# One wait a batch of eight in TensorE's adjacency loop, and one-hot slots of 392 columns in place of 391

## The reference, cut to what matters

```python
edge_index = jnp.stack([src, dst])            # 50000 edges, sorted by dst; 3125 nodes, 128 features
# first network: five gated steps
def step(h, _):
    messages = h[col] @ W_msg.T + b_msg
    agg = jax.ops.segment_sum(messages, row, num_segments=num_nodes)
    ...                                       # gates r, z, n of agg and h
x = _layernorm(x + gated_steps(x))
x = _layernorm(x + edge_network(x, edge_weight))   # three edge layers
```

## Time and profile before

| | us |
|---|---|
| median of 3 runs | 2377.35 (2377.28 to 2377.51) |
| the profiled execution, its own time | 2376.61 |
| the profiled execution, span of its instructions | 2374.4 |
| PE busy in the span | 2020.9 |
| DVE busy | 1455.5 |
| POOL busy | 1063.3 |
| ACT busy | 662.9 |
| adjacency stage: first to last matmul start | 74.1 to 375.7 |
| last staged copy of the stage, opening of the next stage | 379.87, 386.15 |

### The profile page before, as it was taken

One profiled execution on the slowest core, in us unless ns is written; L12 is line 12 of the kernel. 1 busy time (PEld: TensorE's weight loads), 2 busy tenths in 40 slices (PEclk: granted clock), 3 DMA queues, 4 the chain that ended last, 5 costly groups with the idle time before them and its releaser, 6 DMA issues. The chain is left out here.

```text
span 2374.4 us, 50364 instructions
## 1 busy us (share of the span) xinstructions
PE 2020.9 (85%) x14516; PEld 1445.6 (61%) x14516; DVE 1455.5 (61%) x4548; ACT 662.9 (28%) x1344; POOL 1063.3 (45%) x1086
## 2 busy tenths in 40 slices
PE   7687776999999997398888866999999769999983
PEld 4221113454544543287777755999999659888881
DVE  6888873132322323687878846767777467777774
ACT  0145663121211211332333324323233231111111
POOL 0444430000000000377777736777777267777770
PEclk7767767999999998699999978999999889999996
DMA  3022445000000001544444425777777345555541
GB/s 91 14 49 67 87 83 47 0 0 0 0 0 0 0 0 44 209 132 142 143 145 142 144 77 136 210 209 207 209 205 210 93 127 146 146 140 144 142 121 30
DMA packets 188937, 242.83 MB, mean 102 GB/s; under 512 B 53217, under 2 KB 115068, under 8 KB 188076
## 3 DMA queue, kind: packets, MB, share of 16 engines
q1 hardware_dynamic: 155420, 173.31, 25.4%
q0 software_dynamic: 32864, 60.32, 11.1%
q10 hardware_dynamic: 432, 6.29, 0.6%
HBM read 150.92 MB, written 69.26 MB: 93 GB/s over the span
## 5 line engine op out<-in xcount | busy, mean ns | idle before, releaser
L1504 POOL DMA_INDIRECT rows<-p_dram,src_i x912 | 893.0, 979 | 305.1 <-issue 257.4
L1737 DVE TENSOR_TENSOR agg_t<-psum,agg_t 128x128 f32 x1368 | 390.2, 285 | 153.2 <-PE psum L1621 122.9
L1603 PE MATMUL psum<-w_c,before 128*128 128x128 f32 x1824 | 403.6, 303 | 0.0
L1672 ACT ACTIVATE rows<-rows 128x512 f32<-128x512 f32 x228 | 143.7, 630 | 754.6 <-DVE rows L1730 750.5
L884 PE MATMUL psum<-adj,parts 128*128 (+2 forms) x1750 | 339.7, 351 | 5.6 <-ACT agg L963 4.4
L1721 DVE TENSOR_SCALAR hot_w<-col_f,dst_loc,weight 128x128 f32<-128x128 f32 x912 | 319.1, 354 | 0.3
L664 PE MATMUL psum<-src_hot,dst_hot 128*128 128x391 f16 x586 | 228.0, 432 | 81.3 <-ACT psum L686 27.5
L1603 PEld LDWEIGHTS psum<-w_c,before 128*128 128x128 f32 x1824 | 279.7, 194 | 0.0
L1264 POOL MEMSET agg_t<- 128x3200 f32 x1 | 2.8, 2766 | 606.5 <-POOLq L1020 606.5
L1621 PE MATMUL psum<-hot_w,rows 128*128 128x128 f32 x1824 | 247.3, 279 | 29.8 <-ACT rows L1672 25.8
L884 PEld LDWEIGHTS psum<-adj,parts 128*128 128x128 f16 x1750 | 153.0, 98 | 191.1 <-issue 23.4
(11 more groups left out here) (249 smaller groups left out, 2504.3 us busy)
## 6 DMA issues: line engine op xcount, KB each, us to landing
e_dram<-after SPq DMA_DIRECT2D x228, 256.0 KB
before<-e_dram SPq DMA_DIRECT2D x228, 256.0 KB
adj<-stage SPq DMA_DIRECT2D x196, 97.8 KB, 3.5
pair_rows<-sorted_rows SPq DMA_DIRECT2D x114, 128.0 KB, 4.3
rows<-p_dram,src_i POOLq DMA_INDIRECT x912
hot_all<-dst_rows SPq DMA_DIRECT2D x1, 3584.0 KB, 12.5
hot_all<-dst_rows ACTq DMA_DIRECT2D x1, 3072.0 KB, 17.3
hot_all<-dst_rows ACTq DMA_DIRECT2D x1, 2048.0 KB, 10.5
```

Of the source, the lines that this page charges most:

```text
L1504: nc.gpsimd.indirect_dma_start(out=rows[:, b % ROWS, m * D:(m + 1) * D], out_offset=None, in_=p_dram, in_offset=bass.IndirectOffsetOnAxis( ...
L1603: mm = nc.tensor.matmul(o, before[:, q % BEFORE, m * P:(m + 1) * P], w_c[:], start=False, stop=True)
L1672: nc.scalar.activation(e_of(q), source, ACT.Relu).then_inc(e_on, 1)
L1737: nc.vector.tensor_tensor(a, psum[:, A_BANKS[q % len(A_BANKS)], m * P:(m + 1) * P], a, ALU.add).then_inc(agg_on, 1)
```

## The change

The wait for the target batch is made only at the first step of a batch (74 of the 586). The source slots, and the ramp that they are compared with, get 392 columns; the matmul still reads 391 of them.

```diff
+SPAN_COLS = -(-SPAN // 4) * 4
...
-            keep["span_h"] = room[:, 2 * BAND_ROOM:3 * CHUNK].bitcast(F16)[:, 0:SPAN]
+            keep["span_h"] = room[:, 2 * BAND_ROOM:3 * CHUNK].bitcast(F16)[:, 0:SPAN_COLS]
...
-            nc.gpsimd.iota(keep["span_h"], [[1, SPAN]], 0, 0,
+            nc.gpsimd.iota(keep["span_h"], [[1, SPAN_COLS]], 0, 0,
...
-        src_hot = sb("src_hot", [P, MOVES, SPAN], F16)
+        src_hot = sb("src_hot", [P, MOVES, SPAN_COLS], F16)
...
-                pe.wait_ge(dst_on, s // HOT_BATCH + 1)
+                if s % HOT_BATCH == 0:
+                    pe.wait_ge(dst_on, s // HOT_BATCH + 1)
                 pe.wait_ge(src_on, s + 1)
                 pe.wait_ge(free, nth & 255)
                 nc.tensor.matmul(psum[:, bass.ds(bank, 1), 0:SPAN],
                                  dst_hot[:, s // HOT_BATCH % BATCHES, s % HOT_BATCH, :],
-                                 src_hot[:, s % MOVES, :], start=False, stop=False,
+                                 src_hot[:, s % MOVES, 0:SPAN], start=False, stop=False,
                                  skip_group_check=True).then_inc(counted, 1)
```

## The result

| | before, us | after, us |
|---|---|---|
| median | 2377.43 (4 runs) | 2347.06 (2346.03 to 2347.33, 4 runs) |
| profiled execution, its own time | 2376.61 | 2346.03 |
| its span | 2374.4 | 2343.8 |
| first matmul of the stage | 74.1 | 73.9 |
| last staged copy | 379.87 | 347.50 |

The ratio is 0.9869, with a 95% interval of 0.9857 to 0.988: 30.4 us saved, where 29.0 were forecast. Lines behind the change count two higher in the new kernel (L664 is L666, L677 is L679).

A forecast was written before the change was run, and what follows sets the result against it. TensorE's instruction issue bounds the stage's first half, ScalarE very nearly the second. Gain 30.9 - 0.5 - 1.4 = 29.0 us, so 2377.35 - 29.0 = 2348.4 us; range from 2 us below 2344.4 up to 2361.

The forecast's parts named there:

- TensorE is bound by issuing: Weight loads of L664: one every 0.41 to 0.42 us whatever the clock, set by sequencer instructions between loads.
- The price of the wait, 0.105 us at clock 1.0 and 0.089 at 0.5: TensorE's L662 wait: removing it saves this per step, 2.36 us per 28 steps, which fall from 14.22 to 11.86.
- the array's floor: TensorE's load-and-matmul of 391 columns at clock 0.5: no step shorter than 0.326 us.
- A lone wait needs no instruction: Ahead of L663: in 7 of 8 steps the L662 instruction goes, the remaining wait riding on L663's operation.
- ScalarE is next, from the block at 186 us on: Second half of the stage: ScalarE's 14-band blocks can't be shorter than 15.6 or 16.9 us.
- The deductions, 0.5 and 1.4 us: Taken off 30.9 us: VectorE holding TensorE in the first 28 steps, and TensorE and ScalarE delaying each other when level.
- seven blocks: ScalarE's 14-band blocks, 246.7 to 362.8 before: to take ScalarE's own 113.1 us instead of 116.1.
- its own range: Spread of the main forecast's total time: 2344.4 to 2352.8 us.
- level running: TensorE and ScalarE equally fast from about 186 us: each at times loses to the other, 1.4 us taken off.
- The 392 columns at zero: VectorE's source one-hots, L646: widening from 391 columns changes nothing; bounds 0.35 us lost or 0.5 us gained.
- Landings: Rival: staged bands' transfers take over at 0.90 us a band against 0.80, 13 us given back, 2361; chance 0.08.

The follow-up runs named there:

- the run where VectorE never paused: Changed kernel with ScalarE's band ends and TensorE's banks written in as constants, slots of 392 columns: 2844.21 us, ratio 1.0145 to the kernel before.
- the waits of VectorE: Added to the kernel with both engines' constants and 392 columns: VectorE waits each batch, from the third, for GpSimd's scatters; 2322.19 us, ratio 0.9766.

## Why the prediction was right, point by point

- **TensorE is bound by issuing.** Right. Of the three readings in it (the pace ignores the clock, the idle is "issue", the instructions between two loads add up) the two runs with added waits are the test: a second wait instruction moved the pace from 0.415 to 0.52. One figure was weaker than it was read: most of the idle in the 3.24 of 6.00 us is the gap of one register load, 2.56 us from the weight load at 127.80 to the next, and not idle between steps.
- **The price of the wait, 0.105 us at clock 1.0 and 0.089 at 0.5.** The first is right: 0.31 us within a batch, 74 wait instructions. Twenty-eight steps took (199.2 - 84.0) / 10 = 11.5 us between the loads of L655, where the forecast had 11.86 and, with 0.105 throughout, 11.65:

```profile
L655 PEldq TENSOR_LOAD <-band_i x11: 1874/2006/2518, 84.0 to 199.2; - x11
```

  The second was too low. In the stretch of the last row here, at a granted clock of 0.5, the loads still came 0.31 us apart, below the 0.326 that the prediction had as the array's floor:

```profile
88.48 0.10 PEld L666 LDWEIGHTS psum<-src_hot,dst_hot 128*128 128x128 f16 x1 [0.21 <-issue]
88.79 0.10 PEld L666 LDWEIGHTS psum<-src_hot,dst_hot 128*128 128x128 f16 x1 [0.20 <-issue]
89.10 0.10 PEld L666 LDWEIGHTS psum<-src_hot,dst_hot 128*128 128x128 f16 x1 [0.21 <-issue]
...
88.16:89.80 1.64, 1.64 (x6) 0.57 (x6) 0.50 0.25 61
```

  The floor seems to hold over a batch and not for each step: the eight loads from 88.16 on, with the slower first step of a batch among them, took 2.62 us (mean clock 0.55), and 8 x 0.326 is 2.61. By that estimate a batch at 0.5 saves 8 x 0.415 - 2.61 = 0.71 us, where the prediction had 7 x 0.089 = 0.62, and 28 steps save about 2.5 us and not 2.36. The other 0.2 us are not pinned down. The gap at a register load, from the last weight load before it to the first behind it, fell from a mean of 2.59 us (8 gaps before) to 2.46 (10 gaps after), less than single gaps differ by.

- **A lone wait needs no instruction.** Right, but the step's wording (one wait on the operation, "the other became" the instruction) hid a rule that the runs brought out: the wait instruction takes two. So taking one wait out of four ahead of an operation saves an instruction, out of three it saves none, and out of two, as in this kernel, it saves one.
- **ScalarE is next, from the block at 186 us on.** Right. The last load was forecast at 331.9 before deductions, and came at 330.3:

| ScalarE's load, before | forecast | after |
|---|---|---|
| 188.0 | 169.1 | 167.2 |
| 208.6 | 186.3 | 184.8 |
| 226.7 | 201.9 | 200.6 |
| 246.7 | 218.8 | 217.6 |
| 362.8 | 331.9 | 330.3 |

  The run without ScalarE's loads gave 31 us more, so the cap is shown and not only argued.
- **The deductions, 0.5 and 1.4 us.** Both were mis-sized. The 0.5 was too small: in the first 28 steps the loads that open the second, third and fourth batch came 0.85, 0.77 and 0.78 us after the one in front (76.17 to 77.02, 79.24 to 80.01, 82.21 to 82.99) in place of 0.41, so VectorE held TensorE for 1.2 us. The cheaper steps behind them more than made up for it. The 1.4 was a wrong reading: in the block from 296.1 to 314.4 ScalarE waited 0.99 us for a staged band to land, and that is most of the 1.4:

```profile
314.37 0.48 ACT L683 CAST stage<-psum 128x391 f16<-128x391 f32 x1 [0.99 <-DMA adj<-stage]
```

  Where no copy waited so, seven blocks took 112.7 us against my 113.1, in the changed kernel and in the run with the wait alone; with two such waits, in the changed kernel run again, they took 114.8. Two engines running level cost nothing that can be seen; a late landing does, in some executions. Without the deductions the forecast would have been 30.9 us, and the medians of the three pairs gave 30.4, 31.2 (the wait alone) and 31.5 (the changed kernel again). The total came out near for the right reason, ScalarE's own 113.1 us: what was wrong in TensorE's price moved only the point at which ScalarE takes over, by 1.5 us (184.8 against 186.3). The upper end of its own range was also added up wrongly: 29.0 less 3.0 for the seven blocks and less 2.8 for level running at three times its cost is 23.2, which gives 2354.2 and not 2352.8.
- **The 392 columns at zero.** Right, in a run of their own and where VectorE sets the pace. The Trainium skill's rule on 4-byte alignment (VectorE: DVE Perf Modes, section "Mode 2×_1P — pack two bf16 into one 32-bit read") would, as the prediction read it, have made every second slot of 391 slow; 2.98 and 2.99 us for a batch leave no room for that, so here the measurement decides.
- **Landings.** Right that they do not take over. ScalarE waited for a staged band's transfer six times, 2.2 us in all, four of them in the last bands (before: six times, 2.8 us); the other two, 0.20 us at 182.9 and 0.37 at 200.5, lie in mid-stage.
- **A cover that I did not name.** The scatters of GpSimd were counted nowhere. They cost nothing here, yet their mean went from 1134 to 1497 ns, and with VectorE denser still they became the bound. Who is denser after a change, and who shares something with it, belonged in the list of who is late next.

## What to carry to other kernels

Count the sequencer's instructions between two matmuls: where the pace of small matmuls ignores the granted clock, each instruction less is worth its distance to the next one (0.105 us here) and not its own duration (51 ns), and it is instructions that count, not waits. Then follow the next engine block by block before believing the gain; here 50 us on TensorE were worth 30, and the engine that took over was held by its checked register loads, which cost 29 us more and took three lines to change. An engine made to run without gaps can starve another one that looked idle: look at the durations of GpSimd's transfers after every step that makes VectorE denser.

## What the runs showed of the hardware that was not expected

- **One wait instruction of TensorE's sequencer carries two semaphores** beside the one on the next operation: three waits cost as much as two (2377.87 us), the fourth 0.105 us a step. SyncE's eight waits in four instructions say the same of its sequencer.
- **VectorE without gaps can stop a GpSimd transfer for 181 us.** It showed in three steps: a mean of 1134 ns a scatter before, 1497 after, one of 181.25 us in the run where VectorE never paused; with the waits of VectorE it was 18.3 at most. The Trainium skill has the mechanism (SBUF — State Buffer, section "SBUF: two separate sides"): GpSimd writes the descriptors of its own transfers through a port pair that it shares with VectorE, and is locked out while VectorE runs a two-port form. The trace agrees in kind: from the fourth scatter to the fourteenth each ended 0.20 to 0.24 us after a target batch, which is a two-tensor form, had begun, and none during the one-hots. The first two, at 75.99 and 78.10, do not fit: they ended while one-hots were running. That a single scatter can stay out over sixty such batches is more than the page says.
- **A low granted clock can be free.** With two wait instructions the stage had a mean granted clock of 0.50, and its 17.2 us for 28 steps are the 14.22 of before and 28 x 0.105 = 2.94; nothing is left for the clock to have cost. In the changed kernel, steps 0.31 us apart appear at 0.5 as at 1.0.
